# Decoder layers on one core: the value and output weights folded into one matrix per head

## The reference, cut to what matters

```python
def attn_layer(x, Wqkv, qs, ksc, Wo):           # x: 4 x 512 x 128, already token-shifted
    q, k, v = split(x @ Wqkv)                   # 16 heads, 64 wide each
    q = l2norm(q) * qs;  k = l2norm(k) * ksc    # then a rotation with tables
    out = local_attention(q, k, v)              # windows of 32 tokens, each sees itself and the one before
    return out @ Wo                             # 1024 -> 128
def ffn_layer(x, g, bln, W1, b1, W2, b2):
    xn = (x - mean) / sqrt(var + 1e-5) * g + bln
    a, gate = split(xn @ W1 + b1)
    return a * gelu(gate) @ W2 + b2
for i in range(6):
    x = attn_layer(shift_tokens(x), Wqkv[i], q_scale[i], k_scale[i], Wo[i]) + x
    x = ffn_layer(shift_tokens(x), ln_g[i], ln_b[i], W1[i], b1[i], W2[i], b2[i]) + x
```

## Time and profile before

| | us |
|---|---|
| median of three runs | 2065.89 (2062.27 to 2071.86) |
| the profiled execution, its own time | 2066.79 |
| its span | 2065.0 |
| PE busy | 1931.1 (94%) |
| DVE busy | 1519.0 (74%) |
| ACT busy | 1291.1 (63%) |
| POOL busy | 1012.1 (49%) |

### The profile page before, as it was taken

One profiled execution on the slowest core, in us unless ns is written; L12 is line 12 of the kernel. 1 busy time (PEld: TensorE's weight loads), 2 busy tenths in 40 slices (PEclk: granted clock), 3 DMA queues, 4 the chain that ended last, 5 costly groups with the idle time before them and its releaser, 6 DMA issues.

```text
span 2065.0 us, 46724 instructions
## 1 busy us (share of the span) xinstructions
PE 1931.1 (94%) x18988; PEld 1148.6 (56%) x18988; DVE 1519.0 (74%) x1736; ACT 1291.1 (63%) x1824; POOL 1012.1 (49%) x727
## 2 busy tenths in 40 slices
PE   5698887799999999999999999999999999999996
PEld 2121133366666666666666666666666666666663
DVE  4798555687778777877787778777877777777762
ACT  3287734466667666666676667666766676666752
POOL 7100123565556555655565656555655565555530
PEclk9699999899999999999999999999999999999998
DMA  4521010244333443334533434443444343443330
GB/s 107 87 50 25 14 39 6 84 133 105 101 101 101 124 123 101 90 104 121 132 98 97 108 104 132 110 107 90 116 117 128 92 106 100 106 112 99 104 102 19
DMA packets 105349, 195.87 MB, mean 95 GB/s; under 512 B 14096, under 2 KB 34064, under 8 KB 104880
## 3 DMA queue, kind: packets, MB, share of 16 engines
q1 hardware_dynamic: 105136, 192.88, 36.4%
HBM read 124.81 MB, written 54.79 MB: 87 GB/s over the span
## 4 chain that ended last, share of the span: by engine, by line
PE 78%; ACT 2%; issue 1%; DVE 0%; POOL 0%; DMA 0%; SPq 0%; ACTq 0%; POOLq 0%
PE ps L1358 16%; PE ps L1433 9%; PE ps L1388 9%; PE ps L1410 8%; PE ps L1367 8%; PE ps L1443 8%; PE ps L1462 6%; PE ps L1421 4%; PE ps L1398 4%; PE ps L1472 3%; PE ps L1383 2%; ACT l_v_tok L1524 1%; PE ps L1450 1%; POOL l_rot L1331 0%; ACT l_kb L1558 0%
## 5 line engine op out<-in xcount | busy, mean ns | idle before, releaser
L1331 POOL TENSOR_TENSOR l_rot<-l_rot,l_rot_s 128x1024 f32<-128x1024 f32 x192 | 455.2, 2371 | 1.0 <-DVE l_rot_s L1675 1.0
L1320 POOL COPY l_kb<-l_kb 128x512 f32<-128x512 f32 x95 | 62.9, 662 | 685.5 <-ACT l_kb L1558 685.5
L1334 POOL TENSOR_TENSOR l_rot<-l_rot,l_norms 128x1024 f32<-128x1024 f32 x192 | 365.1, 1902 | 15.1
L1663 DVE TENSOR_TENSOR l_rot<-ps,l_tab_c 128x1024 f32<-128x1024 f32 x192 | 234.9, 1224 | 165.4 <-ACT l_sq L1532 165.4
L1532 ACT ACTIVATE l_sq<-ps 128x1024 f32<-128x1024 f32 x192 | 196.8, 1025 | 206.6 <-PE ps L1358 204.0
L1675 DVE TENSOR_TENSOR l_rot_s<-ps,l_tab_s 128x512 f32<-128x512 f32 x384 | 245.5, 681 | 0.0
L1654 DVE TENSOR_REDUCE l_norms<-l_sq 128x16 f32<-128x1024 f32 x192 | 232.1, 1209 | 0.0
L1358 PE MATMUL ps<-l_wqkv,xsT 128*128 128x512 f32 x384 | 187.1, 611 | 16.4 <-ACT l_v_tok L1524 14.0
L1558 ACT ACTIVATE l_kb<-ps 64x1024 f32<-64x1024 f32 x192 | 195.7, 1019 | 1.1
L1410 PE MATMUL ps<-l_vb,l_pT 128*32 128x128 f32 x6144 | 189.4, 274 | 2.8 <-ACT l_pT L1524 1.4
L1388 PE MATMUL ps<-l_kb,l_qT 128*32 128x128 f32 x6144 | 187.6, 274 | 0.0
(11 more groups left out here) (171 smaller groups left out, 3114.3 us busy)
## 6 DMA issues: line engine op xcount, KB each, us to landing
l_vb<-v_scratch SPq DMA_DIRECT2D x336, 256.0 KB, 4.6
v_scratch<-l_v_tok SPq DMA_DIRECT2D x96, 512.0 KB, 4.9
l_vb<-v_scratch SPq DMA_DIRECT2D x48, 192.0 KB, 3.2
xsT<-xT SPq DMA_DIRECT2D x48, 135.8 KB, 2.5
stack<-scratch SPq DMA_DIRECT2D x96, 64.0 KB
l_xf<-xT SPq DMA_DIRECT2D x48, 128.0 KB, 2.4
l_wqkv_odd<-wqkv SPq DMA_DIRECT2D x9, 512.0 KB, 6.4
scratch<-parts SPq DMA_DIRECT2D x12, 256.0 KB, 2.7
```

Of the source, the lines that this page charges most:

```text
L1331: nc.gpsimd.tensor_tensor(rot[:, t % 2, n], rot[:, t % 2, n], rot_s[:, n], ALU.add).then_inc(added, 1)
L1334: nc.gpsimd.tensor_tensor(rot[:, t % 2, n], rot[:, t % 2, n], norms[:, t % 2, n, :, None].broadcast_to([P, HEADS, DH]), ALU.mult).then_inc ...
L1663: nc.vector.tensor_tensor(rot[:, t % 2, 1 - r], slot(name, t).rearrange("p n (h d) -> p (n h) d", d=DH), tab_c[:, 1 - r, t % TILES, None, ...
```

## The change

The product of the value weights and the output weights is formed on the chip, head by head: `fold` multiplies the 64 rows of `wvT` of a head with the 64 rows of `wo` of the same head, 16 matmuls of 128 columns in a layer, and ACT copies the two halves into `l_wvo` (`keep_folded`). A head's value is then 128 wide and already projected. Therefore:

- `project_v` makes 2048 columns instead of 1024: two slots (1 and 2), four matmuls, and ACT makes two copies;
- `store_v` writes 1 MB and not 512 KB, and each full `spread_v` DMA loads 512 KB and not 256 KB; no block of zeros is left in `l_vb`;
- `values` sums the eight pairs in PSUM into one 128x128 tile;
- the probabilities are multiplied by the reciprocal sums on DVE before they are transposed (in `sums`), so `scale_out` becomes a small copy (`keep_out`), `turn_out` one transpose, and DVE adds the transposed tile straight to `xT` (`add_out`), early in the step;
- `project_out` and `copy_out` are gone.

The cut diff:

```diff
         for t in range(STEPS):
-            b_wo, b_norm, b_hid, b_y = pieces(t)
+            _, b_norm, b_hid, b_y = pieces(t)
...
             if has(t):
-                plan(("v", t), 1)
+                plan(("v", t, 0), 1)
+                plan(("v", t, 1), 2)
+            if folded(t) is not None:
+                for parity in range(2):
+                    plan(("f", folded(t), parity), 2 + parity)
...
                 def store_v(t):
-                    wait_free(sp, "v", t)
+                    for parity in range(2):
+                        wait_free(sp, "v", t, parity)
...
                     if b_wo is not None:
-                        wait_free(sp, "wo", b_wo)
+                        wait_free(sp, "oT", (b_wo + 1) * TILES - 1)
...
                 def turn_probs(t):
-                    wait(pe, exped, t + 1)
+                    wait(pe, p_scaled, t + 1)
...
-                            m = nc.tensor.matmul(dst[a:a + WINDOW, c // 4, (c % 4) * P:(c % 4 + 1) * P],
-                                                 pT[:, c, a:a + WINDOW], vb[:, j, :, c * DH:(c + 1) * DH],
-                                                 start=True, stop=True, skip_group_check=True)
+                            m = nc.tensor.matmul(dst[a:a + WINDOW, 0, 0:DIM], pT[:, c, a:a + WINDOW],
+                                                 heads_v[:, j, c * P:(c + 1) * P], start=(c == 0),
+                                                 stop=(c == PAIRS - 1), skip_group_check=True)
...
+                def project_v(t):
+                    b, i = t // TILES % BATCH, t % TILES
+                    for parity in range(2):
+                        if t % NT == 0:
+                            wait_free(pe, "f", t // NT, parity)
+                        take(pe, "v", t, parity)
+                        for c in range(2):
+                            m = nc.tensor.matmul(slot("v", t, parity)[:, c, :], xsT[:, b, PAD + i * P:PAD + (i + 1) * P],
+                                                 wvo_sb[t // NT % 2][:, parity, c * BANK:(c + 1) * BANK],
+                                                 start=True, stop=True)
+                        m.then_inc(filled("v", t, parity), 1)
+                def fold(layer):
+                    wait(pe, wo_ld, 32 * layer)
+                    for parity in range(2):
+                        take(pe, "f", layer, parity)
                     for c in range(PAIRS):
+                        for parity in range(2):
+                            rows = slice(64 * parity, 64 * parity + 64)
+                            m = nc.tensor.matmul(slot("f", layer, parity)[:, c // 4, (c % 4) * P:(c % 4 + 1) * P],
+                                                 wvT_sb[rows, c, :], wo_sb[rows, c, :], start=True, stop=True)
...
                 def copy_v(t):
                     wait(act, v_stored, 16 * t)
-                    copy_slot(("v", t), v_tok[:, :, :])
+                    for parity in range(2):
+                        copy_slot(("v", t, parity), v_tok[:, parity, :].rearrange("p (n x) -> p n x", n=2))
...
                     nc.vector.reciprocal(inv[:, t % 2, :], total[:, t % 2, :]).then_inc(inv_ready, 1)
+                    wait(dve, inv_ready, t + 1)
+                    nc.vector.tensor_tensor(prob[:, t % 2], prob[:, t % 2],
+                                            inv[:, t % 2, :, None].broadcast_to([P, HEADS, 2 * WINDOW]), ALU.mult)\
+                        .then_inc(p_scaled, 1)
+                def keep_out(t):
+                    wait_full(dve, "o", t)
+                    wait_full(dve, "oT", t - 1)
+                    nc.vector.tensor_copy(o_tok[:, :], slot("o", t)[:, 0, 0:DIM]).then_inc(emptied("o", t), 1)
+                def add_out(t):
+                    b, i = t // TILES % BATCH, t % TILES
+                    wait_full(dve, "oT", t)
+                    tokens = xT[:, b, PAD + i * P:PAD + (i + 1) * P]
+                    nc.vector.tensor_tensor(tokens, tokens, slot("oT", t)[:, 0, 0:P], ALU.add).then_inc(emptied("oT", t), 1)
...
                     if has(t - 2):
                         sums(t - 2)
+                    if has(t - 3):
+                        add_out(t - 3)
```

136 lines of the change are left out of this document (60 added, 76 removed).

## The result

The changed kernel takes 2241.09 us (median; 2228.26 to 2246.41), the kernel before 2068.88 beside it (2062.27 to 2080.16). The ratio is 1.0792 [1.0754, 1.0831]. I forecast 2180 with a range of 2100 to 2225: the sign was right, the size too small by 61. The profiled execution took 2243.06 with a span of 2241.2, against 2066.79 and 2065.0.

A forecast was written before the change was run, and what follows sets the result against it. PE's own work was taken as the bound in the layers. Work -53, an old wait gone -10, new waits +181, fold catch-up -4, DMA 0: +114 on 2067, less 1, gives 2180 us, range 2100 to 2225.

The forecast's parts named there:

- that end: DMA queue at 227 GB/s: the store of v, pushed by weight loads past the next copy of v; +45, taken as 0.
- the mean: Norm step: the mean waits for slot 1, which DVE frees with its sine part after `add_out`; 0.86 us.
- signs of being wrong: Changed profile: the forecast is wrong if PE's idle names DMA, the clock falls, or PE's idle before q is absent.
- my own slow end of 9.2: Spread of v: 2 MB would last 9.2 us at 227 GB/s, against 5.6 at 377.
- rival 2: DMA binds because bytes double and the burst already runs at a share of 1.06: +114 + 45, 2225 us; chance 0.13.
- PE's new idle share: Layers: PE waits 8.06 of 72.9 us in four steps, which should not cost clock.
- The chain: Layers: waits for PSUM slots read out by ACT and DVE, 8.06 us per four steps, +181 over 22.5 rounds.
- behind v: Variance, hidden layer and second product wait for ACT to copy v's second half out of slot 2; 1.32 us each.
- q: q waits for slot 2 until DVE's `add_out`: 1.75 us in norm, 0 in hidden, 1.07 in y, 0.42 in out steps.
- The fold: New PE work, 16 matmuls of 128 columns in each of 6 layers: 3.4 us a layer, +20, range 10 to 40.
- won back: Steps with a fold: chains catch up while PE folds, so the next step's waits shrink by 2.2 us; -4 in all.

The follow-up runs named there:

- half the loads: Changed kernel, but each spread DMA loads only half of the value columns from HBM (results not the reference's): 2184.31 us, ratio 1.0527.
- ACT's read-out alone: Changed kernel, but ACT copies the transposed output from slot 2 to SBUF and DVE adds from there: 2221.66 us, ratio 1.071.
- the kernel with `exps` between the copies and 64-partition loads: Changed kernel with batch pieces in slot 0, ACT copying out the transposed output, eight 64-partition loads, and exps between v's two copies: 2120.41 us, ratio 1.0245.
- the three edits together: Changed kernel with batch pieces in slot 0, ACT copying out the transposed output, and eight 64-partition loads: 2130.16 us, ratio 1.0255.

## Why the prediction missed

**The step that failed is DMA.** I wrote "I price that end at 1.9 per round, +45, and take 0, since the pieces will be of the faster kind". Measured: 54.8 in the profiles, 57 in the medians. The mechanism stood in my own text (the shifted copy queues behind the spread, and the mean wants it at about the time it lands). It was also one of my signs of being wrong, that PE's idle names DMA. I set it to nothing by a wrong reading of two rows: in the earlier trace rows I took 227 GB/s as the rate of 2 KB pieces and 377 as that of 4 KB pieces. But the first row is of a load to 32 partitions and the second of the store from 128. The spread's partitions did not change, and so its rate did not. Nor was 377 the trace's best microsecond, as I wrote: from 1712 to 1713 us the store of the kernel before ran at 434, so the limit that I cited there does not hold here. The DMA view of the changed kernel shows loads and store, from 1022 to 1042 us in slices of 0.5 us (busy tenths, then GB/s):

```profile
DMA  9999998998999999999998996100000028997999
GB/s 361 254 238 197 221 189 213 254 221 172 221 238 205 238 172 184 238 266 273 361 374 360 475 410 262 49 0 0 0 0 0 0 82 238 270 147 279 279 246 205
```

Loads in pieces of 4 KB run at about 220 (first two slices apart) up to 1029.5, then the smaller copies of x, and from 1031.5 the store at 360 to 475 up to 1034. The bytes doubled, so the loads take twice as long.

The Trainium skill has the rule that I should have looked up (SBUF — State Buffer, Door 1: The DMA port swizzle): 32 partitions reach 8 of the 16 ports, about 218 GB/s, 64 in one half reach the same 8, and only 128 reach all, 436. This case lies near it in each point: 221, 242, and 381 to 414 GB/s. By it the spread would have lasted 9.6 us (an estimate: 2 MB at 218 GB/s), near my own slow end of 9.2. The Trainium skill's page also says that two transfers to the two halves gain only 6% over one (its section on issuing two DMAs to hit both halves). Here two queues gained more, 273 against 231 GB/s, yet stayed far from the rate of 128 partitions.

So rival 2 was real. I had put it at 2225, the forecast plus 45, with a chance of 0.13. Its price came out at 54.8, and not all of it is the wait that I had priced. Of PE's idle, which grew by 35.2 (191.3 against 156.1 with half the loads), about 18.5 is the mean (30.0 more for the copy, 11.5 less for DVE's sine part) and 14.4 the stops in the values product. The stops had no term in my sum.

**The clock fell behind long waits.** I wrote that PE's new idle share "should not cost clock". Mostly it doesn't, but the waits for DMA reach 2.7 us, longer than any single one in my sum (1.75). The changed kernel's PE, then PE's clock in one-microsecond windows of the same place:

```profile
1103.60 1.98 PE L1375 MATMUL ps<-l_wqk,xsT 128*128 128x512 f32 x4 [1.06 <-DVE xT L1743]
...
1108.73 2.07 PE L1467 MATMUL ps<-l_xf,cst 128*128 128x512 f32 x2 [2.27 <-DMA l_xf<-xT]
```

```profile
1108.00:1109.00 1.00, 0.27 (x1) 0.27 (x2) 1.00 (x2) 0.02 (x1) 1.00 (x1) 0.82 1.01 270
1109.00:1110.00 1.00, 1.00 (x2) 0.23 (x2) 0.26 (x1) 0.00 (x0) 0.92 (x2) 0.50 1.20 365
1110.00:1111.00 1.00, 1.00 (x3) 0.10 (x2) 0.16 (x1) 0.00 (x0) 1.00 (x1) 0.50 1.06 440
```

Behind an idle time of 2.27 us on DMA the granted clock is 0.50, the 1.2 GHz level, for between three and four microseconds, and the mean takes 2.07 instead of 1.1. Summed over all microseconds from 400 to 2160 (one minus the granted clock), 12.0 us of full speed are lost, in seven such places, each behind an idle time of 1.9 to 2.8 us: four behind the shifted copy, two behind stops, one behind ACT's copy of v. Three other idle times of 1.9 to 2.2 us had no such fall behind them. The kernel before lost 0.03 from 400 to 1980, the one with half loads none. With that most of the 54.8 is told: 35.2 is idle, the clock took 12.0, and about 8 stay unassigned. Some versions with a shorter chain lost more to it: 32.4 with ACT's read-out alone, and 25.6 from 400 to 2040, in 14 places, in the kernel with `exps` between the copies and 64-partition loads. With 128-partition loads in that kernel it was 1.7 up to 2000. The falling clock, too, was one of my signs of being wrong.

**The chain was right, step by step.** Start to start in the profile after, what I forecast in brackets: behind v 1.37 (1.32); q reached 5.22 after k in the norm step (5.33), 4.59 in the y step (4.65), 3.88 in the out step (4.00), and no wait in the hidden step (0). Only the mean, 1.8 against 0.86, has another releaser, the DMA. With half the loads it is the one that I named, and the four steps agree to 0.1.

**The fold was sized too high.** I took 3.4, with 1.7 as the low end. PE, in the changed kernel, the first fold and a later one:

```profile
383.23 3.78 PE L1459 MATMUL ps<-l_wo,l_wvT 64*128 64x128 f32 x32 [2.43 <-PEq L729]
386.94 4.42 PE L1375 MATMUL ps<-l_wqk,xsT 128*128 128x512 f32 x8
...
949.06 2.06 PE L1459 MATMUL ps<-l_wo,l_wvT 64*128 64x128 f32 x32 [1.16 <-issue]
951.04 1.98 PE L1375 MATMUL ps<-l_wqk_odd,xsT 128*128 128x512 f32 x4
```

The later ones take 1.98 (949.06 to 951.04), the first 3.71 at a granted clock of 0.50. Six cost 13.6, not 20. The halves of the rows do overlap, as the Trainium skill (TensorEngine Tiling (Array Packing), Theoretical Speedup) has it for a small dimension of 64 (up to twice as fast); against my estimate of 3.44 without overlap it is 1.7 times here. The norm step behind a fold won back 2.0 (19.58 to 17.59 with half the loads), where I had 2.2.

**The early part, +15.6, had no term,** since nothing changes there. It is the clock, as the same 20 us in the kernel before and in the changed one show (the number ahead of the DMA share is the clock):

```profile
240.00:260.00 20.00, 15.78 (x101) 3.72 (x105) 1.84 (x3) 17.40 (x35) 4.53 (x1) 1.00 0.09 16
```

```profile
240.00:260.00 20.00, 18.69 (x69) 2.33 (x68) 1.15 (x2) 11.24 (x22) 0.00 (x0) 0.50 0.09 16
```

Up to 370 us the changed kernel lost 46.1 us of full speed and the kernel before 31.1. It isn't the change's doing: the kernel before with more traffic shows 0.50 there too, and the variants with smaller loads, with the three edits together, with `exps` between the copies and with 128-partition loads alone, all on the changed layers, show 1.00. It differs between executions, and is likely why the runs of one kernel spread by 10 us either way. What decides it stays open. A comparison of two profiles carries this 16 by chance; the price of the loads in the layers alone (54.8) does not depend on it, and the medians give nearly the same (57).

In sum, between the profiles: 15.6 early clock, 3.7 first fold, 104.5 chain less saved work, 54.8 with the loads, -2.4 at the end, together 176.2.

## What to carry to other kernels

Before you give a DMA rate to a transfer, ask how many partitions it reaches, and take the rate from a row of a transfer with the same reach; a faster row of the same trace may differ in direction, piece size and partitions at once. A wait that you add and a transfer that you make longer don't cost their separate prices: each repair of the chain gave back a part to the late copy, and idle times of about two microseconds often brought a slower clock on top. When a row of your own gives a cost (+45) and a guess takes it away, keep the cost in the sum: here each step of the chain was right to a quarter of a microsecond, and the total was still off by 61.

## What the runs showed of the hardware that I had not expected

- The same bytes in the same pieces load at 221 GB/s into 32 partitions at a time, at 242 into 64 and at 381 to 414 into 128. Two queues on the two halves of SBUF reached 273 where both ran, against 231 and 213 for one alone.
- Within the values product PE stopped with no releaser in the trace, 9 to 29 times in each kernel with slow full loads, up to 2.8 us each and 10.5 to 31.4 in all. With half the loads it was under 2 us in all, with fast full loads in the best order 8.0. The traces show a link. Each of the 15 stops of the changed kernel ended 1.2 to 1.5 us after the end of a 16 KB packet of the queue that the page names "instruction" (q8, 148 packets in 2241 us). So did, at 1.1 to 1.65 us, 201 of the 214 stops in all profiles, but only 12% of the other instructions of the changed kernel's values products. This points to PE waiting for its own instructions. No run changed that queue's work by itself, so how the loads hold it up stays open.
- The granted clock fell to 0.50 for between three and four microseconds behind seven of the ten idle times of 1.9 to 2.8 us on PE, in a kernel that kept PE busy for 87% of its span.
